# A two-stage vision block on one core: the copied planes of the packed convolution's second tile, one column to the left

## The reference

```python
x = x + attn_out                                         # 96 channels, 32 x 32
hdn = conv1x1_bn(x, w1, s1, b1)                          # 96 -> 384 channels
hdn = lax.conv_general_dilated(hdn, wdw, window_strides=(1, 1), padding=((1, 1), (1, 1)),
                               feature_group_count=HID) + bdw[None, :, None, None]
hdn = jax.nn.relu(hdn)
mlp_out = conv1x1_bn(hdn, w2, s2, b2)                    # 384 -> 96 channels
return x + mlp_out
```

## Time and profile before

| what | value |
|---|---|
| median of three runs | 6548.63 us (6542.64 to 6558.43) |
| the profiled execution's own time | 6551.87 us |
| its span, first to last instruction | 6550.1 us |
| busy over the span | TensorE 92%, VectorE 81%, GpSimd 72%, ScalarE 58% |
| attention stage | first convolution matmul at 94.6 us, last at 1745.1 us |

### The profile page before, as it was taken

The page is one execution under the profiler, slowest core; times in us unless marked ns, Lnnn a source line. Parts: engine busy times, 40 slices in busy tenths (PEclk is TensorE's granted clock), DMA queues, the critical chain, the costliest instruction groups (busy, mean ns, idle before and its releaser), DMA issues. The chain is left out here.

```text
span 6550.1 us, 228395 instructions
## 1 busy us (share of the span) xinstructions
PE 6045.6 (92%) x96947; PEld 3504.6 (54%) x96947; DVE 5288.5 (81%) x7881; ACT 3770.7 (58%) x5658; POOL 4727.5 (72%) x3268
## 2 busy tenths in 40 slices
PE   6999999999699999999999998999999999998799
PEld 2444444444255655555655555655555656655343
DVE  5666666666588888888888888888888888888687
ACT  3544545445256666656666665666665666665676
POOL 2444444444278888878888888888888888888577
PEclk9999999999899999999999999999999999999899
DMA  1111111111100000010000000000001000000322
GB/s 34 44 47 50 50 43 47 47 47 51 48 3 3 3 3 3 3 45 3 3 3 3 3 26 22 3 3 3 3 3 45 3 3 3 3 3 12 97 82 63
DMA packets 115658, 157.65 MB, mean 24 GB/s; under 512 B 30512, under 2 KB 79952, under 8 KB 114768
## 3 DMA queue, kind: packets, MB, share of 16 engines
q1 hardware_dynamic: 114768, 144.38, 7.7%
HBM read 53.67 MB, written 52.79 MB: 16 GB/s over the span
## 5 line engine op out<-in xcount | busy, mean ns | idle before, releaser
L323 ACT ACTIVATE nn_yy<-nn_P 128x612 f32<-128x612 f32 x1200 | 816.9, 681 | 1612.2 <-DVE nn_P L379 1594.3
L445 PE MATMUL nn_P<-nn_hh,fw_w 64*64 64x256 f16 x38400 | 1535.1, 273 | 217.3 <-DVE nn_nl L390 105.5
L291 POOL TENSOR_TENSOR nn_hf<-nn_hf,nn_sr 128x512 f32<-128x512 f32 (+1 forms) x800 | 1439.9, 1820 | 156.1 <-DVE nn_sr L412 156.1
L302 POOL TENSOR_TENSOR nn_hl<-nn_hf,nn_hh 128x512 f16<-128x512 f32 (+1 forms) x768 | 1266.6, 1649 | 311.6 <-ACT nn_hh L335 302.8
L445 PEld LDWEIGHTS nn_P<-nn_hh,fw_w 64*64 64x64 f16 x38400 | 1020.8, 106 | 833.6 <-issue 661.8
L452 PE MATMUL nn_P<-nn_nh,nn_w 64*64 64x512 f16 x19200 | 1315.9, 379 | 80.6 <-DVE nn_nl L390 10.0
L379 DVE SCALAR_TENSOR_TENSOR nn_P<-nn_P,nn_xs 128x612 f32<-128x612 f32 x1200 | 960.9, 801 | 231.5 <-PE nn_P L445 205.6
L385 DVE TENSOR_TENSOR nn_P<-nn_P,nn_nh 128x612 f32<-128x612 f32 x1200 | 960.4, 800 | 213.1 <-ACT nn_nh L328 206.3
L445 PE MATMUL nn_P<-nn_hl,fw_w 64*64 64x256 f16 x19200 | 992.4, 270 | 3.0 <-issue 2.9
L390 DVE SCALAR_TENSOR_TENSOR nn_nl<-nn_P,nn_nh 128x612 f16<-128x612 f32 x1200 | 952.4, 794 | 34.4
L328 ACT ACTIVATE nn_nh<-nn_yy 128x612 f16<-128x612 f32 x1200 | 856.1, 713 | 37.9
(11 more groups left out here) (222 smaller groups left out, 7875.7 us busy)
## 6 DMA issues: line engine op xcount, KB each, us to landing
xn_scratch<-at_xb SPq DMA_DIRECT2D x128, 114.8 KB
nn_xs<-xn_scratch SPq DMA_DIRECT2D x48, 306.0 KB, 3.2
at_x<-in_x SPq DMA_DIRECT2D x32, 384.0 KB, 3.7
x_scratch<-at_x SPq DMA_DIRECT2D x64, 192.0 KB, 2.1
h_scratch<-nn_hf SPq DMA_DIRECT2D x48, 256.0 KB, 3.0
ml_xt<-x_scratch SPq DMA_DIRECT2D x32, 384.0 KB, 4.2
ml_ht<-h_scratch SPq DMA_DIRECT2D x128, 96.0 KB
out<-ml_ot SPq DMA_DIRECT2D x64, 192.0 KB, 3.3
```

The costliest lines, as they stand in the source:

```text
L291: e.tensor_tensor(hf[c][:, g, :], hf[c][:, g, :], sr[c][:, :].unsqueeze(1).broadcast_to((128, g.stop - g.start, A_COLS)), ALU.mult).then_i ...
L302: e.tensor_tensor(hl[c][:, g, :], hf[c][:, g, :], hh[c][:, g, :], ALU.subtract).then_inc(h_lo[n], 1)
L323: e.activation(half(yy[k % RING][:, :]), Pv[k % 2], ACT.Ln).then_inc(logged, 1)
L445: return pe.matmul(out[:, 0:AC, rows_y] if near else out[:, 1:BC, rows_y], w1[rows, wp, a, 1 if near else 0, k, cols], (hh, hl)[dp][u][row ...
```

## The change

The copies into `xq` take the plane from one element further on, and the matmuls on `xq` read from column 0 in place of column 1. The two together read the same pixels as before. Nothing else is changed: the number and order of the instructions on TensorE, VectorE, ScalarE and GpSimd is the same, and on the DMA queue the two copies into `xq` have the same place, with 1,155 and 1,154 elements for each partition in place of 1,156 and 1,155.

```diff
@@ -662,7 +662,7 @@
         xr = [[sb(f"xr{p}_{h}", [128, HW + 2, HW + 2], F16) for h in (0, 1)] for p in (0, 1)]
         ones16 = sb("ones16", [1, HW, HW], F16)
-        PACKED = [(xp, dy, 0, 128) for dy in range(3)] + [(xq, dy, 1, 128) for dy in range(3)] + [(xr, 0, 2, 96 + TAPS)]
+        PACKED = [(xp, dy, 0, 128) for dy in range(3)] + [(xq, dy, 0, 128) for dy in range(3)] + [(xr, 0, 2, 96 + TAPS)]
@@ -749,7 +749,7 @@
             def pack(m, q, T, h):
                 need(e, (s_x1_hi, s_x1_lo)[h], 2 * m + 2)
                 plane = lambda t_, lo, hi: t_[q][h][lo:hi].rearrange("p r c -> p (r c)")
-                for dst, lo, hi, source, shift in ((xp, 96, 128, 0, 1), (xq, 0, 64, 32, 0), (xq, 64, 128, 32, 1), (xr, 0, 32, 0, 0), (xr, 32, 64, 0, HW + 2), (xr, 64, 96, 0, 2 * HW + 4)):
+                for dst, lo, hi, source, shift in ((xp, 96, 128, 0, 1), (xq, 0, 64, 32, 1), (xq, 64, 128, 32, 2), (xr, 0, 32, 0, 0), (xr, 32, 64, 0, HW + 2), (xr, 64, 96, 0, 2 * HW + 4)):
                     n_ = (HW + 2) * (HW + 2) - shift
                     e.dma_start(plane(dst, lo, hi)[:, 0:n_], plane(xp, source, source + hi - lo)[:, shift:shift + n_]).then_inc(s_packed[q][h], 16)
```

## The result

| | before | after |
|---|---|---|
| median | 6551.24 us (6542.64 to 6558.43, 6 runs) | 6525.08 us (6522.84 to 6533.72, 6 runs) |
| the profiled execution's own time | 6551.87 us | 6529.80 us |
| its span | 6550.1 us | 6528.0 us |
| first to last convolution matmul's row | 94.6 to 1745.1 us | 95.0 to 1722.5 us |
| median of a matmul on `xp` / `xq` / `xr` | 379 / 392 / 379 ns | 379 / 379 / 379 ns |

The changed kernel is faster, by well under 1%. The ratio of its runs to those of the kernel before is 0.9963, with a 95% interval from 0.995 to 0.9976, which is 16 to 33 us. The two profiled executions differ by 22.1 us, and the time from the first to the last convolution matmul went from 1650.5 to 1627.5 us.

The account below looks back on a forecast made before the run. TensorE's dense matmul stream was taken to bound the attention stage. 22.4 us, less a little at the ends, gave 22: 6551.87 - 22 = 6529.9 profiled, 6526.6 against the median 6548.63, stated as 6527 us; range 6515 to 6540.

Parts of the forecast that it names:

- What bounds the stage: Attention stage: TensorE busy 400.00 of 400.00 us, bound by what each matmul takes from start to start, no wait between.
- 13 ns for each of 1,724: Matmuls on `xq` at the full clock: each gains 392 - 379 = 13 ns, together 22.4 us.
- The term of 22.4 less a little: Gain of the `xq` matmuls, 22.4 us, less a little lost at the stage's ends, taken as 22 us.
- The four at half clock: Four of 1,728 `xq` matmuls, one at 97.1 us and three at 1743.78, where the clock is half: no gain.
- The loss at the ends: Filling and emptying pipeline: two images of 32 at 0.7 us each at risk, at most 1.4 us.
- The waits: Close waits of TensorE on other engines: each has at least four times what it loses, so nothing charged.
- The four spare times: Cover before `e_sum` 0.61 us, `mix` 0.58, `project` 0.96 and the next image's `conv` 2.9.
- The copies at nothing: Copies into `xq` starting one element further: cost 0, between -0.1 and +0.1 us on a copy.
- rival 1: The 13 ns on `xq` matmuls belong to the tile, not the column: time 6549 us; chance 0.09.
- rival 2: Part of the gain turns into waits at four close places, paying back 13 of 22 us: 6540 us; chance 0.06.
- rival 3: Copies into `xq` land late and `conv` waits once per image: 6563 us or more; chance 0.03.
- The rule of the number of columns alone: Skill's Back-to-back issue gap: 216 ns per 512-column matmul at full clock, first column free, so gain 0, time 6549 us.

Follow-up runs that it names:

- the first four experiments: Against the kernel before: shifted copies alone, 6545.24 us; column 0 reads alone, 6521.05. Against the changed kernel: `xp` from column 1, 6547.85; `xr` from column 1, 6532.6.

## Why the prediction was right

- **What bounds the stage.** Right, and tested both ways: 22.4 us taken out of TensorE's matmuls shortened the time from the first to the last convolution matmul by 23.0 us, to 1627.5 where 1628 was forecast, and putting the price on `xp` gave it all back (1650.0 us).
- **13 ns for each of 1,724.** Right. The medians say 13 (392 to 379), six starts say 0.07 us / 6 = 11.7. The term of 22.4 less a little stands against 22.1 us between the two profiled executions. That the gain comes with the reading column, and not with the copies or the tile, is shown by the first four experiments.
- **The four at half clock gain nothing.** The last three `xq` matmuls after the change still take 1.28 us, in the view below, as the three on `xp` do.

```profile
1719.94 1.49 PE L1192 MATMUL at_PC<-at_xp,at_w1T 128*128 128x512 f16 x3
1721.22 1.49 PE L1192 MATMUL at_PC<-at_xq,at_w1T 128*128 128x512 f16 x3
1722.50 0.63 PE L1192 MATMUL at_PC<-at_xr,at_w1T 105*128 105x512 f16 x1
```

- **The loss at the ends, up to 1.4 us.** Charged at 0.4; the trace shows none.
- **The waits.** The four spare times were to shrink by 0.10, 0.01, 0.12 and 0.16 us. They went from 0.61 to 0.51, 0.58 to 0.57, 0.96 to 0.84 and 2.9 to 2.7, and the idle time behind them stayed, 17.7 us before and 16.9 after.
- **The copies at nothing.** Right by the median landing times and by the run with the copies alone. Single copies took up to 4.3 us, 0.6 more than before; the wait for them is 1.5 us in the whole run and was 1.7.
- **The rivals.** The tile (rival 1) is refuted by `xp` and `xr` at 392 ns from column 1. Waits in place of the gain (rival 2) and late copies (rival 3) are not seen in the trace.
- **The rule of the number of columns alone.** By it nothing would have been gained. It fails here: 512 columns take 379 or 392 ns, and 496 columns take the 379 ns of 512. The Trainium skill, TensorE: Matmul & The Clock Gate, Step-by-step: what each phase is for, gives 216 ns for 512 columns of matmuls back to back; the section that the prediction names has the same formula for a matmul by itself.
- **The time.** 6527 was forecast, and the median is 6525.08. By the medians the gain is 26.2 us, 4 more than the trace accounts for. The runs of the kernel before spread over 16 us and the interval begins at 16 us of gain, so these 4 us need no cause. Nor is it more than luck that the profiled execution, forecast at 6529.9, took 6529.80: the kernel that only reads from column 0 has its last `xq` matmul at 1722.6 us, against 1722.1 in the changed one, and its profiled execution took 6522.27.
- **The mechanism was told too narrowly.** The prediction named rows that begin off a multiple of 4 bytes. What is paid for is the number of 4-byte words that a row touches: rows of 31 from column 1 also begin off a word, touch 16 words, and cost nothing. For rows of 32 the two say the same, so the forecast did not suffer.

## What to carry to other kernels

When a stage is bound by a dense stream of matmuls, compare the start-to-start distance of matmuls of one shape, tile by tile: where 16-bit operands are read in rows, a row that begins in the middle of a 4-byte word and ends in the middle of another costs one more word. This was measured for float16 rows of 31 columns and more; rows of 16 cost more than that unless each began on a multiple of 16 bytes, and no run had another element size. If the data is copied into place anyway, choose the copy so that the rows begin on a word. Before counting such a gain, look at what waits: the spare time of a wait shrinks by the shortened work between the start of its chain and its end, not by the gain of a whole pass.

## What the runs showed of the hardware that was not expected

- The distance between matmuls at the full clock (2.4 GHz), for float16 rows of 31 columns and more, follows words and not columns: 256 words (16 rows of 32 from column 0) take 217 ns, 257 words (one run of 512 from an odd element) 217, 264 words (8 rows) 223, 272 words (16 rows) 228. By the medians, 16 words more cost 13 ns, 0.8 ns a word, which is about two cycles of that clock for the two columns of a word. A matmul of 496 columns in 256 words takes the 379 ns of one of 512.
- Rows of 16 columns cost more than their words when they lie across 16-byte pieces: with 256 words, 379 ns on the pieces, 386 at 8 bytes past, 395 with rows 68 bytes apart, so that their starts take every place in turn. Rows of 32 columns, 68 bytes apart as well, have no such surplus (379 ns).
- At half clock (1.2 GHz) the extra word is not seen: three on `xq` take 1.29 us and three on `xp` 1.28. These three of each are all that the reading rests on.
